# Two graph layers on one core: the second norm's output turned by DMA, residuals and turned first norm in two tiles each, and a new order of the dense products

## What is computed

```python
h = jnp.maximum(_layernorm(x), 0.0)
x = x + _L0(h, adj, Wq, bq, Wk, bk, Wv, bv, Wo, bo)   # 16 heads of 32, masked softmax
h = jnp.maximum(_layernorm(x), 0.0)
x = x + _L1(h, adj, weight, wq, wk)

# _L1:
output = h @ weight
alpha = (h @ wq) @ (h @ wk).T
alpha = jnp.maximum(alpha, 0.0) * (graph != 0)
alpha = jax.nn.softmax(alpha, axis=1)
return alpha @ output
```

## Time and profile before

| | |
|---|---|
| median of three runs | 1569.95 us (1569.84 to 1571.14) |
| the profiled execution, its own time | 1570.8 us |
| its span, first to last instruction | 1569.0 us |
| PE busy in the span | 1504.6 us |
| DVE / ACT / POOL busy | 1247.9 / 1128.3 / 1064.8 us |
| mean granted TensorE clock | 0.992 |

### The profile page before, as it was taken

The page is one execution under the profiler, slowest core; times in us unless marked ns, Lnnn a source line. Parts: engine busy times, 40 slices in busy tenths (PEclk is TensorE's granted clock), DMA queues, the critical chain, the costliest instruction groups (busy, mean ns, idle before and its releaser), DMA issues.

```text
span 1569.0 us, 50846 instructions
## 1 busy us (share of the span) xinstructions
PE 1504.6 (96%) x16561; PEld 1106.7 (71%) x16561; DVE 1247.9 (80%) x4042; ACT 1128.3 (72%) x2477; POOL 1064.8 (68%) x1478
## 2 busy tenths in 40 slices
PE   2889999999999999999999999999999999999996
PEld 1557777777777777777777777777777777777753
DVE  6778888887887878788888878888887888888763
ACT  2567777777777777777777777777777777777761
POOL 2466767777677777767677776777776777777650
PEclk9999999999999999999999999999999999999998
DMA  7647777667667766666776766777676677767760
GB/s 241 135 95 132 133 163 160 152 136 152 138 138 166 160 144 143 144 136 148 166 157 141 152 140 134 154 160 159 135 158 136 133 161 160 153 135 159 125 119 16
DMA packets 656198, 226.28 MB, mean 144 GB/s; under 512 B 611488, under 2 KB 627872, under 8 KB 656160
## 3 DMA queue, kind: packets, MB, share of 16 engines
q1 hardware_dynamic: 636848, 188.57, 59.1%
q10 hardware_dynamic: 19312, 37.23, 8.5%
HBM read 57.94 MB, written 16.78 MB: 48 GB/s over the span
## 4 chain that ended last, share of the span: by engine, by line
POOL 35%; issue 34%; PE 22%; DVE 4%; ACT 2%; DMA 1%; POOLq 1%; SPq 0%; ACTq 0%; DVEq 0%
PE ring L408 18%; POOL wv_raw L1115 16%; POOL heads_out L1149 6%; POOL x L1172 4%; POOL keep L1181 3%; POOL far L1190 3%; POOL xa L1137 1%; PE score L464 1%; PE pv L483 1%; DMA turned<-wv_raw 1%; POOL newton L1133 1%; PE ring L518 1%; PE pv L485 0%; DVE wk_raw L864 0%; DVE tops L785 0%
## 5 line engine op out<-in xcount | busy, mean ns | idle before, releaser
L1115 POOL TENSOR_TENSOR wv_raw<-wk_raw,wv_raw 128x512 f16<-128x512 f32 x512 | 608.0, 1190 | 362.8 <-ACT wv_raw L638 358.5
L625 ACT ACTIVATE wk_raw<-wk_raw,least 128x256 f32<-128x256 f32 x1024 | 459.0, 497 | 6.8 <-DVE least L864 6.8
L864 DVE CUSTOM_DVE_ANT_0 wk_raw<-score,far,undo_score 128x256 f32<-128x256 f32 x1024 | 444.0, 478 | 7.1 <-issue 5.1
L638 ACT ACTIVATE wv_raw<-wk_raw 128x512 f16<-128x512 f32 x512 | 320.5, 626 | 8.6 <-issue 4.5
L483 PEld LDWEIGHTS pv<-val,turned 128*128 128x128 f16 x2048 | 149.7, 97 | 67.4 <-issue 43.9
L483 PE MATMUL pv<-val,turned 128*128 128x65 f16 x2048 | 185.9, 192 | 10.8 <-DMA turned<-wv_raw 7.0
L408 PE MATMUL ring<-wv_hi,h 128*128 128x256 f16 x1024 | 189.3, 273 | 0.0
L408 PE MATMUL ring<-h,wq_hi 128*128 128x256 f16 x1024 | 176.3, 274 | 7.6 <-DVE wk_lo L827 7.6
L1149 POOL TENSOR_TENSOR heads_out<-o_sum,o_rcp 128x64 f32<-128x64 f32 x512 | 153.0, 320 | 42.6 <-DVE o_sum L879 42.6
L485 PE MATMUL pv<-val,turned 128*128 128x33 f16 x2048 | 178.1, 179 | 0.0
L408 PE MATMUL ring<-h,wk_hi 128*128 128x256 f16 x1024 | 176.6, 274 | 0.0
(11 more groups left out here) (151 smaller groups left out, 3570.6 us busy)
## 6 DMA issues: line engine op xcount, KB each, us to landing
xin<-x_dram ACTq DMA_DIRECT2D x32, 512.0 KB, 3.8
out_dram<-xo SPq DMA_DIRECT2D x32, 512.0 KB, 3.7
xa<-x_dram ACTq DMA_DIRECT2D x31, 512.0 KB, 4.2
adj_in<-adj_dram SPq DMA_DIRECT2D x32, 256.0 KB, 2.9
turned<-wv_raw SPq DMA_TRANSPOSE x512, 3.2
adjt_in<-adj_t_dram SPq DMA_DIRECT2D x32, 256.0 KB, 3.1
wq_raw<-wq_dram SPq DMA_DIRECT2D x2, 512.0 KB, 7.0
wk_raw<-wk_dram SPq DMA_DIRECT2D x2, 512.0 KB, 8.6
```

What stands on the lines that cost most here:

```text
L625: last = nc.scalar.activation(probs[:, at, q, :], probs[:, at, q, :], ACT.Exp, bias=least[:, at, q:q + 1], scale=-1.0)
L638: nc.scalar.activation(halves[:, at, :, 0, :], probs[:, at, :, :], ACT.Copy).then_inc(hi["p"], 1)
L864: last = nc.vector.tensor_tensor_reduce(out=probs[:, at, q, :], in0=score[u % GROUP][:, q * NODES:(q + 1) * NODES], in1=far[:, q, :], scal ...
L1115: nc.gpsimd.tensor_tensor(halves[:, at, :, 1, :], probs[:, at, :, :], halves[:, at, :, 0, :], ALU.subtract).then_inc(lo["p"], 1)
```

## The change

`DENSE` has a new order. `qk0` and `qk1` of the next graph stand at steps 6 to 8, in front of `g0` (steps 8, 9) and `g1` (9, 10); `hw0` is at 10 and 11, `al` at 12, `hw1` at 13, `v0` at 14, `av0` at 15, and `av1` moves to step 0 of the following body. The last two bodies have orders of their own. The tiles `h2_0` and `h2_1` are gone: ACT and DVE make the halves of the second norm from `work` in SBUF into `half2`, and SP issues two DMA transposes into `h2`, at steps 5 and 6. `h1` exists twice, by the parity of the graph, and its two transposes stand at steps 3 and 5. The residual exists twice too: the last product is added in place and stored from there (`xo` is gone), and the store stands at step 9. The start-up (which loads come first, the scales, the merging of `wm`) is dealt out anew.

```diff
 DENSE = [
-    ["qk2a"],
+    ["av1", "qk2a"],
     ["wo0a", "ot1", "qk2b"],
     ["wo0b", "wo1a"],
     ["wo1b"],
     ["qk3"],
-    ["v1a", "h2_0", "h2_1", "v1b"],
-    ["g0"],
-    ["g1a"],
+    ["v1"],
+    ["qk0a", "qk0b"],
+    ["qk1a"],
+    ["qk1b", "g0a"],
+    ["g0b", "g1a"],
     ["g1b", "hw0a"],
-    ["hw0b", "qk0a"],
-    ["qk0b", "ala"],
-    ["alb", "ot0"],
+    ["hw0b", "ot0"],
+    ["al"],
     ["hw1"],
-    ["qk1"],
-    ["v0a", "av0"],
-    ["av1", "v0b"],
+    ["v0a", "v0b"],
+    ["av0"],
 ]
+DENSE_LAST = [[name for name in step if name not in ("ot0", "av0")] for step in DENSE]
+DENSE_LAST[14] = DENSE_LAST[14] + ["ot0"]
+DENSE_END = [[], ["wo0a", "ot1", "av2"], ["wo0b", "wo1a"], ["wo1b", "av5"], [], [], [], ["g0"], ["g1"],
+             [], [], [], ["al"], ["hw0"], ["hw1"], ["av0", "av3"]]
...
 AL_STEP = step_of("al")
+SOFTMAX_STEP = AL_STEP + 1
-STATS1, ROOT1, NORM1, LATE_MASK = (8, 9), 10, 12, 5
-XA_STEP, SCALE_STEP = 5, 6
-HIGH1_STEP, LOW1_STEPS, TURN1_STEP = 14, (0, 2), 6
-VAR2 = 4
+STATS1, ROOT1, NORM1, LATE_MASK = (8, 9), 10, 13, 5
+XA_STEP, SCALE_STEP = 5, 5
+HIGH1_STEP, LOW1_STEPS, TURN1_STEPS = 15, (0, 2), (3, 5)
+VAR2, TURN2_STEPS = 4, (5, 6)
...
             # SP
+            def transpose_h2(q, b):
+                if started(b - 1):
+                    sp.wait_ge(mm["hw"], count(b - 1, 2, 1))
+                    settle(sp, sp_settled)
+                    sp.wait_ge(mm["al"], count(b - 1, 1, 0))
+                    settle(sp, sp_settled)
+                sp.wait_ge(lo["h2"], count(b, QT, q))
+                settle(sp, sp_settled)
+                sp.dma_start_transpose(
+                    h2[:, :, :, q * P:(q + 1) * P].rearrange("p h d n -> p (h d) n"),
+                    half2[:, q, :, :].rearrange("p h d -> p (h d)")).then_inc(h2_in, 16)
...
                     head = ahead(s, TURN_AHEAD, t, cur, nxt)
                     if head:
                         transpose_probs(*head)
-                    if s == TURN1_STEP and nxt:
-                        transpose_h1(n)
+                    if s in TURN1_STEPS and nxt:
+                        transpose_h1(TURN1_STEPS.index(s), n, 1 - odd)
+                    if s in TURN2_STEPS and prev:
+                        transpose_h2(TURN2_STEPS.index(s), p)
...
             # ACT, in body
                     if head:
                         exponentials(*head)
-                    if s == AL_STEP + 1 and prev:
+                    if soften and cur:
                         second_high(p)
-                    for name in DENSE[s]:
+                    if s == VAR2 and prev:
+                        for q in range(QT):
+                            second_half(q, p)
+                    for name in deal(t)[s]:
...
             # DVE, in body
-                    if s == AL_STEP + 1 and prev:
+                    soften = prev and s == SOFTMAX_STEP
+                    if soften:
                         second_reciprocal(p)
                     for by in MASKS_AHEAD[s % GROUP][:1 if s == LATE_MASK else 2]:
                         head = ahead(s, by, t, cur, nxt)
                         if head:
                             mask(*head)
                     if s == VAR2 and prev:
                         reciprocal_deviation(p)
-                        second_normalise(p)
-                    if s == AL_STEP + 1 and prev:
+                        second_normalise(p, residual[1 - odd])
+                    if soften and cur:
                         second_low(p)
+                    if s == VAR2 and prev:
+                        for q in range(QT):
+                            second_half(q, p)
```

More of the change, by code:

```diff
@@ L113, in started, with deal, order @@
     return not (isinstance(graph, int) and graph < 0)
+def deal(t):
+    if isinstance(t, int) and t >= BATCH - 1:
+        return DENSE_LAST if t == BATCH - 1 else DENSE_END
+    return DENSE
 def bank_before(name, t):
-    at, shift = ORDER.index(name), 0
+    def order(body):
+        return [other for step in deal(body) for other in step if not other.endswith("b")]
+    body, at = t, order(t).index(name)
     while True:
@@ L121, in bank_before @@
         if at < 0:
-            at, shift = at + len(ORDER), shift - 1
-        other = ORDER[at]
+            body -= 1
+            at = len(order(body)) - 1
+        other = order(body)[at]
+        graph = body + ROLE[other]
         if BANK[tile(other)] != BANK[tile(name)]:
             continue
-        graph = t + shift + ROLE[other]
-        if t + shift == 0 and tile(other) in SPARE:
+        if body == 0 and tile(other) in SPARE:
             return other, -1 - t
-        if t + shift < -1:
+        if body < -1:
             return None, 0
@@ L337, in _ @@
             sp.dma_start(xa[:], x_v[0, :, :, :]).then_inc(xa_in, 16)
+            for half in range(2):
+                load_raw(sp, "wq", half)
             sp.dma_start(bias_q[:], bq).then_inc(small_in, 16)
@@ L426, in merge @@
             def merge(at, other, off):
-                dst = ring[BANK[SPARE[at]]]
-                s, per, idx = RELEASE[tile(other)]
-                pe.wait_ge(s, count(off, per, idx)) if off >= 0 else pe.wait_ge(
-                    merged_out, SPARE.index(tile(other)) + 1)
-                if at > KT:
-                    turn_tops(2, dst)
-                    spread_scale(2, 3, dst)
-                    return
-                if at < KT:
-                    cols = slice(at * P, (at + 1) * P)
+                dst, job = ring[BANK[SPARE[at]]], JOBS[SPARE[at]]
+                if other is not None and off < 0:
+                    pe.wait_ge(merged_out, SPARE.index(tile(other)) + 1)
+                elif other is not None:
+                    s, per, idx = RELEASE[tile(other)]
+                    pe.wait_ge(s, count(off, per, idx))
+                batch = BATCH_OF.get(SPARE[at])
+                if job == "turn":
+                    turn_tops(batch, dst)
+                    return
+                if job == "spread":
+                    spread_scale(batch, 2 if batch == 2 else 1, dst)
+                    return
+                if job == "bias":
+                    for half in range(2):
+                        wait_raw(pe, "wo", half)
+                    for k in range(KT):
+                        last = nc.tensor.matmul(dst[:], bv_wide[:, k, :], raw["wo"][:, k, :],
+                                                start=(k == 0), stop=(k == KT - 1))
+                else:
+                    cols = slice(job * P, (job + 1) * P)
                     for half in range(2):
@@ L579, in dense, with body @@
                             ).then_inc(mm["av"], 1)
[L581 to L582 removed]
+            def body(t, odd, prev, cur, nxt, later):
+                present = {-2: prev and started(t - 2), -1: prev, 0: cur, 1: nxt}
                 for s in range(HEADS):
@@ L596, in body @@
                         spread_scale(0, 2, pv)
-                    if nxt and not cur and s == step_of("qk0") - 1:
+                        for _ in range(WARM):
+                            nc.tensor.matmul(ring[1][:, 0:P], ident[:], ident[:], start=True,
+                                             stop=True)
+                    if nxt and not cur and s == step_of("qk0"):
                         turn_tops(1, pv)
-                    if nxt and not cur and s == step_of("qk0"):
-                        spread_scale(1, 1, pv)
                     if s in SCORE_STEPS:
@@ L766, in body @@
                         act.dma_start(xa[:], x_v[n + 1, :, :, :]).then_inc(xa_in, 16)
+            for half in range(2):
+                load_raw(act, "wk", half)
             act.wait_ge(const_ok, 2)
```

339 lines of the change are left out of this document (187 added, 152 removed).

## The result

The changed kernel took 1826.61 us in the median of four runs (1818.57 to 1837.22), the kernel before beside it 1570.55. The ratio is 1.1634, with a 95% interval of 1.1573 to 1.1694. The prediction, 1578 us within 1543 to 1598, was right in its sign and wrong by 249 us in its size. The profiled execution took 1837.22 us.

What follows compares the result with a forecast made beforehand. PE alone was taken to set the period: 44.75 + 0.9 + 1.15 = 46.8 us a body, 24.5 us more over 29 bodies, less 13 (start) and 2.5 (end), 9 us more: 1578 us, 8-in-10 range 1543 to 1598.

Steps and rivals of the forecast that it cites:

- PE's own work: PE's steady body without waits: 45.96 us less 1.2 for the dropped transposes of `work` and a wait, 44.75 us.
- the fourth rival: The dropped PE transposes of `work` were worth twice what their starts show, with both stalls: 1545 us; chance 0.03.
- The first norm's second transpose: In front of `qk0a`: leaves SP at 13.4, lands by 17.2 against a use at 17.4, so no cost.
- rival A: Experiment on earlier first-norm transposes: the transfer waits for its data, not its queue place; gain under 10 us; no chance given.
- The stall at `av0`: Second layer's softmax: `hw_lo` lets PE start 7.0 us behind `al`, PE has 5.9 of work; stall 1.15 us a body.
- Head 7 and the DMA: Weighing of head 7 at step 8: its turned head lands behind load `xa` at 23.1; stall 0.9 us a body.
- The start and the end: PE's time without work: 13 us regained of 44.6 at the start, 2.5 of 17.7 at the end.

Runs made afterwards that it cites:

- a_straight_turn1: Changed kernel without a hardware loop, the first norm's two transposes issued at steps 2 and 3 instead of 3 and 5: 1631.8 us.
- a_best23: Changed kernel without loop; first norm's transposes at steps 2 and 3, `al` half a step earlier, DVE's second mask behind sum, `e_lo`, `hw_lo`: 1610.4 us.
- b_straight: Kernel before with no hardware loop, its 28 middle bodies written out one behind the other: 1590.6 us.
- a_straight_turn1_al: Changed kernel without loop, first norm's transposes at steps 2 and 3, `al` moved earlier in all bodies but the first graph's: 1621.1 us.
- b_two: Kernel before with only its loop changed, two bodies written out in each of 14 iterations: 1663.3 us.
- b_four: Kernel before with only its loop changed, four bodies in each of 7 iterations: 1637.2 us.

## Why the prediction was wrong

**PE's own work.** Right: 44.75 us a body predicted, 44.84 and 44.91 shown. The transposes were worth what their starts said, and the fourth rival falls.

**The loop.** The failed step is none of the sum's terms but one that it lacks. The full diff has a loop of two bodies with step 2 for the parity of the tiles (`engine.Fori(2, BATCH - 3, 2)`, which the section on the change does not mention); I costed the parity at nothing and never asked what the doubled code does. Without the loop the changed kernel is 136 of the 256 us faster.

**The first norm's second transpose.** Failed: "cost nothing", with its landing at 17.2 before a use at 17.4. A margin of 0.2 us on a chain of a dozen hand-overs was no ground for zero. In the body that begins at 759.36 PE came to `qk0` 17.4 us behind the first weighing, as forecast, but the transpose had been issued at 15.9 and not 13.4, and `qk0` waited 1.6 us. SP issues it in its order, behind turned heads. Putting the two transposes one and two steps earlier in that order gave 59 us, where rival A, that the half itself is late, allowed less than 10.

**The stall at `av0`.** The chain was right: without the doubling `hw_lo` ends 7.0 us behind `al` (690.84 to 698.74, less 0.9), where 6.9 was predicted. The wait was put at the wrong instruction. Behind `hw_lo` in DVE's order stands the sum of heads 12 and 13 (0.5 us), and the weighing before `av0` needs it: 1.63 us in `a_straight_turn1` where 1.15 was predicted. I named what is queued behind the wait on PE, not what is queued behind `hw_lo` on DVE. In the changed kernel the doubling of `e_lo` makes it 2.54.

**Head 7 and the DMA.** The chain was right, the stall failed: 0.9 us a body predicted, in the 29 bodies 2.0 us in 3 waits measured in front of head 7 and 7.4 in 6 in front of head 8, and 13.4 us for all turned heads of the run. `a_straight_turn1`, without the gaps and the wait for `h`, shows why. SP turns head 7 at 18.85 in most bodies (18.9 predicted) and it lands at 22.9 in the median (23.1 predicted), but PE comes at 23.2 and not at 22.4, since it has waited before, mostly for heads 4 and 5, which the prediction did not look at. Head 7 waits there for 3.5 us in 6 bodies, all turned heads for 19.1. What the second norm's transposes cost is 0.4 us a body.

**The start and the end.** Both failed. The weighing that ends the first stretch stands at 155.62 where it stood at 151.63: 4.0 us lost where 13 were forecast as regained. PE's wait of 7.6 us for `wk_lo` has shrunk to 0.9, but the waits for sums of heads (`o_sum`) are 9.8 us there (before 3.5), one wait that nothing in the profile ended is 6.2 (before 1.5) and those for `h` are 3.8; the longest, for a transfer that DVE issued, is 18.6 (before 19.5). From the same weighing of the last full body to the end it is 89.1 us and was 84.0: 5.1 lost where 2.5 were forecast as regained. The waits for `hw_lo` (4.6 us) did go. But the last graph waits 9.1 us for the second norm's transposes, where 3.8 were waited for the norm itself, and the prediction had given their DMA 3 us.

**The clock.** Not in the prediction at all. PE's busy time grew by 45 us though it has 237 matmuls fewer. In the windows shown the clock fell in a gap of 4.4 us and cost another 2.5 us of work by the estimate above; the prediction costed every wait at its bare length.

What stays open: of the 41 us that `a_best23` takes more than before, writing the bodies out has 24 and the second norm's transposes 21 to 26, against 32 that PE saves. That leaves some 23 to 28 us, mostly weighings that wait for turned heads more often than in `b_straight` (59 times against 37). They are new in front of heads 0 and 1: in the 29 bodies PE waits for these 0.5 us in `b_straight`, 13.5 in `a_straight_turn1_al` and 24.3 in `a_best23`. No run tells the cause.

## What to carry to other kernels

When a change unrolls a hardware loop, count the code of one iteration first: look for the bytes on the instruction queues and for gaps in which every engine stands still, and price each iteration, here 5 to 7 us beyond the same bodies written out. When an operation moves on an engine that works in order, list what is queued behind it there and who waits for that, and which operation of VectorE with two SBUF operands now meets one of GpSimd's. A step whose input lands 0.2 us before its use is a coin toss, not a zero.

## What the runs showed of the hardware

- The loop of 28 iterations of one body fetched 0.34 MB on instruction queue `q8`, the other forms 2.15 to 2.75 MB, in 16 KB pieces, whether they paused or not. PE stood still at each jump back in a loop of two or four bodies: 13 times in `b_two` (3.5 us in the mean), 6 times in `b_four` (3.4), 13 times in the changed kernel (4.5).
- In the gap that began at 701.7 the granted clock was 1.00 up to 704 and 0.56 from 704 to 706. PE had work again from 706.08, and the clock was 0.50 up to 710 and 1.00 from 712.
- An `e_lo` of 0.40 us and a low half of 1.11 us side by side pass one for one, at 1.29 us each. `hw_lo`, with one operand in PSUM, takes 9.66 us for 16 with and without low halves beside it.
- A delay of 0.4 us in front of `e_lo` made the kernel 34 us slower; in 30 graphs the second `e_lo` moved into that meeting and took 1.38 us.
